# First mixer of a two-layer decoder: norms, casts, squares and scalings on ScalarE, context rounding on VectorE instead of GpSimd, new orders

## The reference

```python
xn  = layernorm(x) * gamma + beta
q,k,v = split(xn @ W_in + b_in)            # then rotary on half of k and v
k, v  = k / norm(k), v / norm(v)           # cosine normalisation per token
a     = sum over tokens of k * v           # one number per channel
x1  = layernorm(2 * x + (q * (0.5 + 0.5 * a)) @ W_out + b_out)
# context product: both sides rounded to fp8 values with block scales
w   = fp8_rounded(ctx^T, blocks of 128 x 128)   # scale: max over a whole block
xq  = fp8_rounded(x1, blocks of 1 x 128)
x2  = layernorm(x1 + xq @ w)
top 8 of 64 experts of x2 @ gate_w, softmax weights
slot[token, k] = region of the expert (2048 rows each) + place of the token in it
```

## Time and profile before

| | |
|---|---|
| median of 3 runs | 2405.23 us (2404.15 to 2417.76) |
| profiled execution | 2399.88 us, its span 2398.2 us |
| granted TensorE clock, mean | 0.885 |
| busy PE, DVE, ACT, POOL | 1819.3, 1687.7, 754.8, 1266.4 us |
| first mixer, until the slot table is read back | 549.6 us of the span |

### The profile page before, as it was taken

How to read it: one execution, slowest core, us unless ns; L and a number is a source line. 1 busy time by engine, 2 the same in 40 slices (tenths; PEclk the granted TensorE clock), 3 DMA queues, 4 the chain that set the end, 5 groups by cost and what they waited for, 6 DMA issues and landing times. The chain is left out here.

```text
span 2398.2 us, 37746 instructions
## 1 busy us (share of the span) xinstructions
PE 1819.3 (76%) x8830; PEld 1436.8 (60%) x8831; DVE 1687.7 (70%) x3189; ACT 754.8 (31%) x1479; POOL 1266.4 (53%) x860
## 2 busy tenths in 40 slices
PE   5797868325999999999984998787510599899990
PEld 4565555114888888888873565554310487788770
DVE  6779585845777877778852166868685588787865
ACT  2121112002444444444432244434220243344340
POOL 2315656744677777777760101535274476576770
PEclk9898878657999999999996999999755699999995
DMA  6010011015887788888855102020100587788865
GB/s 243 19 50 21 7 64 36 1 36 162 205 210 200 200 222 211 224 201 216 227 117 218 36 1 88 18 70 1 53 15 21 165 209 212 205 212 215 221 138 211
DMA packets 139055, 310.63 MB, mean 130 GB/s; under 512 B 35582, under 2 KB 36094, under 8 KB 137588
## 3 DMA queue, kind: packets, MB, share of 16 engines
q1 hardware_dynamic: 68500, 196.50, 24.3%
q0 software_dynamic: 68384, 109.29, 22.8%
q10 hardware_dynamic: 2112, 4.19, 0.5%
HBM read 242.90 MB, written 99.45 MB: 143 GB/s over the span
## 5 line engine op out<-in xcount | busy, mean ns | idle before, releaser
L93 POOL DMA_INDIRECT tab_rows<-pair,slot x256 | 311.6, 1217 | 265.5 <-DVEq L1971 114.5
L1164 POOL DMA_INDIRECT xg<-x_rows,ids x270 | 349.8, 1296 | 105.0 <-issue 88.9
L85 PE MATMUL gu<-wgu_h,xgT_h 128*128 x1040 | 375.6, 361 | 11.2 <-DVE xgT_l L1337 3.2
L85 PE MATMUL gu<-wgu_l,xgT_h 128*128 x1040 | 352.5, 339 | 0.0
L85 PE MATMUL gu<-wgu_h,xgT_l 128*128 x1040 | 350.9, 337 | 0.0
L1173 POOL DMA_INDIRECT acc_rows<-ysb,ids x128 | 221.0, 1727 | 146.1 <-ACT ysb L1217 66.0
L1173 POOL DMA_INDIRECT odd_rows<-ysb,ids x128 | 225.3, 1760 | 122.3 <-issue 41.9
L1217 ACT ACTIVATE ysb<-yp,wts 128x512 f32<-128x512 f32 x256 | 176.2, 688 | 246.6 <-PE yp L1431 200.3
L1337 DVE TENSOR_TENSOR xgT_l<-tpx,xgT_h 128x512 fp32r<-128x512 f32 x262 | 180.1, 687 | 76.1 <-ACT xgT_h L1203 58.8
L85 PEld LDWEIGHTS gu<-wgu_h,xgT_h 128*128 128x128 f32 x1040 | 197.6, 190 | 30.1 <-issue 27.3
L1321 DVE TENSOR_TENSOR wgu_l<-wgu_sb,wgu_h (+1 forms) x112 | 197.2, 1761 | 24.3 <-issue 22.9
(11 more groups left out here) (422 smaller groups left out, 3969.5 us busy)
## 6 DMA issues: line engine op xcount, KB each, us to landing
wgu_sb<-in_wgu SPq DMA_DIRECT2D x112, 768.0 KB
wd_sb<-in_wd SPq DMA_DIRECT2D x112, 256.0 KB
wd_sb<-in_wd SPq DMA_DIRECT2D x112, 128.0 KB
odd_rows<-zero SPq DMA_DIRECT2D x2, 4352.0 KB, 14.6
ct<-in_ctxT SPq DMA_DIRECT2D x8, 1024.0 KB
xg<-x_rows,ids POOLq DMA_INDIRECT x270
xb<-in_x SPq DMA_DIRECT2D x4, 1024.0 KB
x_rows<-mag SPq DMA_DIRECT2D x4, 1024.0 KB
```

The lines of the kernel that those rows point to most:

```text
L85: i = nc.tensor.matmul(out, left(k), right(k), start=(start and k == 0 and m == 0), stop=(k == ops - 1 and m == 2))
L93: nc.gpsimd.indirect_dma_start(out=tab, out_offset=bass.IndirectOffsetOnAxis(ap=s["slot"][:, n:n + 1].bitcast(U32), axis=0), in_=s["pair"] ...
L1164: nc.gpsimd.indirect_dma_start(out=xg[:, t % G, :], out_offset=None, in_=x, in_offset=bass.IndirectOffsetOnAxis(ap=ids[:, t:t + 1].bitcast ...
```

## The change

What it does, part by part:

- The three layernorms keep their statistics on VectorE, but the scaling is done by ScalarE (`layernorm_scales`, `layernorm_act`, both there already for the second mixer).
- GpSimd keeps only the all-reduce and the scatter. `2 x` is made by ScalarE (`doubled`); the output bias becomes a row of `bkv_s` that a matmul adds in `out`; the context is rounded by VectorE (`context_rounded`), with both scalings by ScalarE.
- The scalings of x1 and of the context around the rounding are 16 ScalarE instructions of 128x128 each (`scaled_blocks`) in place of one 128x2048 product on VectorE or GpSimd.
- The fp32r cast of the transposed xn goes to ScalarE; the squares are taken from PSUM right after each copy, so that the PSUM bank is free only after them (`kv_product` waits on `s_sq`).
- One-hots are bf16 with the expert as the outer dimension, as in the second mixer.
- Orders: `context_scales` moves ahead of `context_added` and `scaled_q`; `norm1(a+1)` ahead of `norm3(b)`; the transposes of the next xn come between `out(a,1)` and `out(a,2)`, those of x2 behind `out(a,3)`.

```diff
+def scaled_blocks(nc, dst, src, scale, ready):
+    for n in range(16):
+        nc.scalar.activation(dst[:, n, :], src[:, n, :], ACT.Copy, scale=scale[:, n:n + 1]).then_inc(ready, 1)
...
             def step(b, a, more):
                 if a is not None:
...
                     nc.gpsimd.partition_all_reduce(amw2[:, :], amw[:, :], P, bass.bass_isa.ReduceOp.max).then_inc(s_amr, 1)
-
-                    pool.wait_ge(s_in, a * 16 + 16)
...
-                    c.done(nc.gpsimd.tensor_tensor(res[:, :, :], xb[:, :, :], bout[:, :].unsqueeze(1).to_broadcast([P, BT, D]), ALU.add))
-                    fence()
-                    nc.gpsimd.tensor_tensor(res[:, :, :], res[:, :, :], xb[:, :, :], ALU.add).then_inc(s_rin, 1)
...
-                    rounded(nc.gpsimd, c, fence, wq[:, :, :], sw, wscr, wmag).then_inc(s_wq, 1)
...
             def kv_taken(a, j):
                 act.wait_ge(s_kvp, a * BT + j + 1)
                 nc.scalar.copy(kv[:, j, :], mm[:, 2 * (j % 2):2 * (j % 2) + 2, :].rearrange("p a n -> p (a n)")).then_inc(s_kve, 1)
+                act.wait_ge(s_kve, a * BT + j + 1)
+                for h in range(2):
+                    nc.scalar.activation(mm[:, 2 * (j % 2) + h, :], mm[:, 2 * (j % 2) + h, :], ACT.Square,
+                                         accum_out=ssq[:, 2 * j + h:2 * j + h + 1]).then_inc(s_sq, 1)
...
+                if b is not None:
+                    normed(1, c_n2, b, x1, res, s_x1)
+                doubled(a, b)
+                for j in range(HEAD, BT - 1):
+                    kv_taken(a, j)
+                    if b is not None and j == HEAD:
+                        act.wait_ge(c_qu, b * 9 + 5)
+                        act.wait_ge(s_x2f, b + 1)
+                        scaled_blocks(nc, scr, x1[:, :, :].rearrange("p j (k m) -> p (j k) m", m=P), rsx, s_scr)
+                kv_taken(a, BT - 1)
+                if b is not None:
+                    act.wait_ge(c_qu, b * 9 + 9)
+                    scaled_blocks(nc, scr, scr, sx, s_xq)
...
+                if more:
+                    roots[0].give(act, a + 1, stats[0][2][:, :])
...
+                    layernorm_act(nc, xn, xb, stats[0][2], stats[0][3], s_xn)
+                if b is not None:
+                    normed(2, c_n3, b, x2, x1, s_x2)
+                if b is not None:
+                    scaled_blocks(nc, wscr, wscr, rsw, s_ctu)
+                if more:
+                    transposed(a + 1)
...
+                act.wait_ge(c_sc, a * 8 + 8)
...
+                scaled_blocks(nc, wq, wscr, sw, s_wq)
...
             def step(b, a, more):
                 if b is not None:
                     norm2(b)
-                    quantise(b)
-                if a is not None:
-                    context_max(a)
-                    rotate(a)
-                if b is not None:
+                context_max(a)
+                if b is not None:
+                    quantise_scales(b)
+                if b is None:
+                    context_scales(a, True)
+                rotate(a, 0, 1)
+                if b is not None:
+                    quantise_rounded(b)
+                rotate(a, 1, BT)
+                if b is not None:
+                    context_scales(a, False)
                     context_added(b, 0)
                     context_added(b, 1)
-                if a is not None:
-                    scaled_q(a)
+                scaled_q(a)
...
                 if b is not None:
                     context_added(b, 2)
+                if more:
+                    norm1(a + 1)
+                if b is not None:
                     context_added(b, 3)
                     norm3(b)
-                if a is not None:
-                    context_scales(a, b is None)
-                if more:
-                    norm1(a + 1)
-                if a is not None:
-                    residual(a)
+                residual(a, 0, 2)
                 if more:
                     split_xnT(a + 1)
+                residual(a, 2, BT)
+                context_rounded(a)
...
             def out(a, j):
+                nc.tensor.matmul(mm[:, j, :], one[:, :], bkv_s[:, 2 * D:3 * D], start=True, stop=False)
...
+                if more:
+                    normed(a + 1)
                 if a is not None:
                     out(a, 2)
                     out(a, 3)
+                if b is not None:
+                    transposed(lambda j, k: x2[:, j, k * P:(k + 1) * P], tb, s_x2, BT, s_x2p, s_x2e, b)
```

398 lines of the change are left out of this document (180 added, 218 removed).

## The result

The changed kernel took 2409.43 us (median of 12 runs, 2394.93 to 2418.95), the kernel before 2398.47 us beside it (12 runs, 2384.99 to 2417.76): a ratio of 1.0059, 95% interval 1.0033 to 1.0085. Run again in a later set as a control it came out at 1.0035 (1.0009 to 1.0060). So it is slower by about half a per cent. The forecast was 15.6 us more, +0.65%. Its time, 2420 us, stands 10.6 us above the measured one, and 6.8 us of that is the kernel before, whose median was 2405.23 us in the 3 runs that the forecast started from and 2398.47 in these 12.

The account below looks back on a forecast made before the run. No engine is full; VectorE stretching under GpSimd's work and GpSimd's queue make steps long. Terms −5 + 3 + 9 + 12.6 − 4 = +15.6 take 2399.9 to 2415.5, plus 5.3 for the median: 2420 us, range 2384 to 2438.

Parts of the forecast that it names:

- The gate: Steps 2 and 3: the moved context scales wait for the all-reduce behind the scatter; rinv moves from 36.8 to 58.2 us.
- Rival A: Steps 2 and 3: all-reduce done by about 36 us, so rinv comes 21.5 us earlier; 2377 us, chance 0.15 (below 2381).
- Its weaker form: Steps 2 and 3: with VectorE idle, scatter transfers run at 1.28 us throughout, 5.4 us off each step; 2409 us.
- Steps 2 and 3: Second and third loop steps: +9 and +12.6 us, to 128.0 and 113.2, with the all-reduce ending 55.8 us in.
- The other reckoning: Scatter in steps 2 and 3: by the skill's port rule, dropping two VectorE products returns nothing; each step 2.6 us longer.
- Step 1: First full step: 17.9 us less GpSimd stretching against 21.3 more ahead of the logits; +3, 115.7 to about 119 us.
- Tail: Last scatter with the change of block, up to the slot table's read: unchanged at 47.0 us, transfers issued at 1.28 each.
- Step 0: Up to the next batch's first product: ScalarE scales xn and GpSimd computes nothing; −5 us, 106.5 to 101.6.
- drained: Drained step to its first slots: norms add 2 x 0.9, half the waits without releaser come back; −4, 60.7 to about 57.
- Scaling: ScalarE's 128x128 scalings: 0.31 us start to start, 5.0 for 16, range 0.2 to 0.5; wrong if under 0.2 or over 0.45.
- Rival B: ScalarE's queue, twice on the chain, becomes the bound and the result is slower: above 2429 us, chance 0.21.
- Rival C: Step 1: larger GpSimd relief, ScalarE's work hidden under products, about 106 us; 2407 in all, chance 0.62 shared with the forecast.

Follow-up runs that it names:

- no_scatter: Changed kernel with the three scatters inside the steps left out; steps 2 and 3 took 110.8 and 92.1 us (total of 2365.79 us not to be compared).
- late_again: Changed kernel with VectorE's context scales back behind norm3 and ScalarE's wait for them just ahead of the context scalings; 2390.75 us, ratio 0.9908 to the kernel before.
- early_scales_old: Kernel before with only the four small context scales moved ahead of the two first context additions on VectorE; 2443.73 us against 2417.43, ratio 1.0104.
- blocks_after: Changed kernel with ScalarE's 16 context scalings moved behind its four pairs for the next batch's transposes; 2400.95 us, ratio 0.9975 to the kernel before.
- switch_early: Changed kernel with one small unread iota on GpSimd right behind the last all-reduce; 2423.19 us, ratio 1.0044 to the kernel before.
- first set: Four kernels run beside the kernel before (2417.43 us): two variants moving context scales, one taking the all-reduce first, one adding a small iota; ratios 1.0014 to 1.0104.
- second and third set: Later runs beside the kernel before (2406.71 and 2407.43 us): the unaltered changed kernel, at ratio 1.0035, and variants of it.

## Why the prediction was right, and where its terms were off

The forecast was that the change gives as much as it takes, because moving four small instructions puts VectorE's queue behind GpSimd's scatter. The result and the runs bear out both.

*The gate.* All-reduce behind the scatter, VectorE's 18 to 22 us of idling (17.17), TensorE's wait, the low clock after it: all found. The narrow matmuls take 6.98 us after it, as before (6.99), and 3.73 without it. `no_scatter` and `late_again` price it at 23.5 and 25.0 us in steps 2 and 3 together, `early_scales_old` at 25 us (1.04% of 2417) on the old kernel, a stretched `rinv` in step 1 included. Rival A (the wait does not bind) falls: it needed `rinv` by 36 us into the step, and it came at 51.8. Its weaker form gave 2409 us, the very time measured, but by a scatter of 1.28 us a transfer; the 32 transfers took 46.0 us, 1.44 each, as forecast (1.45). That agreement is chance.

*Steps 2 and 3, forecast 128.0 and 113.2, found 122.9 and 105.2.* The mis-sized term is the all-reduce's end, forecast 55.8 us into the step: it ended after 49.3 and 48.7. Its part "+ 6.4" was the unexplained gap ahead of the all-reduce in the earlier trace rows, and it goes with GpSimd's elementwise work ahead of the scatter, which the change took away: 8.48 and 7.56 us with it, 7.70 and 7.48 in `early_scales_old`, which keeps that work, 1.88 and 1.58 without. Behind the all-reduce the sums of 72.2 and 57.4 us measured 73.6 and 56.5.

*The scatter.* The 2.6 us that the forecast gave back, for two VectorE products fewer under it, were 2.3: from its first transfer to its last it took 48.3 us before and 46.0 now. The other reckoning in the prediction, by which nothing comes back and the time is 2425 us, does not hold.

*Step 1, forecast 119, found 122.3 and 120.8.* From the first product of the batch to the end of the logits it was 105.1 us, 23.9 more than before, where 21.3 was forecast; the rest took 17.2 instead of 16.6. Up to the transposes of the quantised x1 it was 4.7 us more than before (41.6 against 37.0), where +7 less 1.5 was forecast; TensorE waited 4.07 us for its PSUM banks, not 5.5. The first part of the forecast was thus right in kind and a little large. What was put too low lies behind the context products: from their end to the end of the logits it was 38.0 us, 17.6 more than before, where 13.5 and 2 were forecast. There `blocks_after` undoes 6.0 us by shortening TensorE's 7.06 us wait. The forecast also held this wait to be some 12 us; it was 7.06 and, ahead of output 2, 2.24.

*Tail, forecast 47.0 unchanged, found 54.0.* This term was missed, and 7.0 us were put at nothing. "Its 32 transfers are issued at 1.28 us each, whoever wrote the slots" holds, but the block behind them begins with an iota, and GpSimd's last work other than transfers had been an all-reduce. `switch_early` moves the price and takes it out again.

*Step 0, forecast 101.6, found 102.6; drained, forecast 57, found 54.5.* The scaling of xn on ScalarE and the absence of GpSimd's rounding did what was said. The drained step lost the holes without a releaser altogether, not by half; as they come and go with the execution, that is no gain of the change.

*Scaling.* Estimated at 0.31 us start to start, found 0.30: 16 in 4.80 us. Rival B, whose sign was over 0.45, falls. The group by line and shape:

```profile
L162 ACT ACTIVATE ct<-ct,rsw 128x128 f32<-128x128 f32 x64 | 19.1, 387 | 0.0
L434 ACT ACTIVATE mm<-mm 128x512 f32<-128x512 f32 x32 | 18.7, 585 | 0.5
...
L434 ACT ACTIVATION_READ_ACCUMULATOR mm<-mm 128x1 f32 x32 | 6.1, 190 | 0.0
```

So the sum, +15.6 in the mixer, was +11.9 (561.5 less 549.6). It would be larger but for 6.3 us less in the drained step, where the profile of the kernel before had its holes. Steps 2 and 3 were put 13.1 us too high, step 1 and the tail 10.3 too low, steps 0 and drained together 1.5 too high. The total is right partly by luck, because errors of opposite sign offset one another. The larger ones are the same thing: GpSimd's price for a change of work, which left the steps (5.98 to 6.6 us in each of two) and came back in the tail (7.0).

*Rival C (a larger relief) is true of the parts.* With its three misplacements mended, the same work runs in 515 us, 34 less than before (6.3 of them in the drained step, where the holes were). That is the worth of all parts of the change together; no run separates the relief of GpSimd from the rest.

## What to carry to other kernels

Before an instruction is moved up in an in-order queue, look at what it waits for and at everything queued behind it: four 0.2 us instructions cost 25 us, most of it because their operand came from behind a 46 us scatter. Where an all-reduce and a long scatter share GpSimd, put first the one that somebody waits for. Read effects of half a per cent from the marks of the stretch that was edited, and run the unaltered kernel beside the edits.

## What the runs showed of the hardware

- GpSimd idles some 7 us when it goes from an all-reduce to elementwise work or an iota, and some 6 to 6.6 us more than otherwise the other way. Between the all-reduce and `res` it was 6.88 us in step 2 of the kernel before:

```profile
287.44 4.50 POOL L404 TENSOR_TENSOR res<-xb,bout 128x2048 f32<-128x2048 f32 x1 [6.88 <-issue]
```

  It was 6.76 in `switch_early`, and 9.40 against 2.47 ahead of the iota of the next block. The other way it was 8.48 against 1.88 and 7.56 against 1.58 ahead of the all-reduce. Between all-reduce and indirect transfers it was 0.57 us. What GpSimd does in that time no run shows.
- A VectorE instruction can be stretched by GpSimd's elementwise work: `rinv`, 128x4 numbers, took 4.29 us beside GpSimd's addition for `res` in `early_scales_old` and 0.16 in the kernel before. No VectorE instruction was seen stretched like this in the steps of the changed kernel, where GpSimd computes nothing elementwise.
- Waits of 1.7 to 17 us without a releaser, on ScalarE, VectorE and TensorE, many at nearly the same moments, were in every profile of the first set, and in the drained step of the one profile of the kernel before. None was in the profiles of the changed kernel or in those of the second and third set, with the same program on the same chip among them. Their cause stays open. The drained step was up to 18 us longer with them, and they fill the very stretch in which a wait is being measured.
- A scatter's transfers took 2.53, 2.74 and 2.02 us instead of 0.97 while VectorE ran its four 128x2048 operations from 241.5 to 248.7 us, two of one operand and two of two. The Trainium skill (SBUF — State Buffer, "Who interferes with whom") ties this to the operations that take the shared write port and exempts sums of two tensors, which it calls inferred. The second and third of these transfers ran beside the sums alone (from 244.05 us), so the trace doesn't agree. VectorE's two reductions over 128x2048 at 229.37 and 232.41 us left the transfers at 0.97.
- A table load on ScalarE took 1.28 us in the rows above, with the next instruction 0.02 us behind it and the one before 0.02 us ahead. The Trainium skill (ScalarE: Activation LUTs, "What ACT_TABLE_LOAD costs") gives about 1283 ns, which agrees, and adds a drain of about 1.38 us to each; no such pause is in this trace.
